# FFN weights quantized in their final work space, later modulation rows in two stages, sigmoid ahead of the small loads, new fill and drain orders

## The reference, cut to what matters

```python
mod = (_silu(L0_c) @ L0_wmod).reshape(B, 6, 1, -1)
sa, ca, ga, sb, cb, gb = (mod[:, i] for i in range(6))
ga = (2 * (ga >= 0) - 1) * max(abs(ga), 0.25)        # gb likewise
h = _layernorm(x) * (1 + ca) + sa
x = x + ga * rwkv_two_layers(h)     # each layer: _time_mix (wkv scan over 4096 tokens), then _channel_mix
h = _layernorm(x) * (1 + cb) + sb
x = x + gb * fp4_ffn(h)             # gate, up, down, inputs and weights quantized in blocks of 16
...
# fp4_quant_dequant(w): scale = max|block| / 6, values rounded to {0, .5, 1, 1.5, 2, 3, 4, 6}, times scale
```

## Time and profile before

| | us |
|---|---|
| median of 3 runs | 2996.9 (2995.78 to 2999.09) |
| profiled execution, its own time | 2993.3 |
| its span | 2991.6 |
| PE busy in the span | 2765.8 (92%) |
| DVE, ACT, POOL busy | 2360.4, 1382.2, 1283.5 |

### The profile page before, as it was taken

One profiled execution on the slowest core, in us unless ns is written; L12 is line 12 of the kernel. 1 busy time (PEld: TensorE's weight loads), 2 busy tenths in 40 slices (PEclk: granted clock), 3 DMA queues, 4 the chain that ended last, 5 costly groups with the idle time before them and its releaser, 6 DMA issues.

```text
span 2991.6 us, 78855 instructions
## 1 busy us (share of the span) xinstructions
PE 2765.8 (92%) x32829; PEld 2201.4 (74%) x32829; DVE 2360.4 (79%) x5345; ACT 1382.2 (46%) x2771; POOL 1283.5 (43%) x1457
## 2 busy tenths in 40 slices
PE   5789999999999999999999999999999999999875
PEld 3567777777777777777777777777777777777653
DVE  5756888888888888888888888888888888888664
ACT  1344444544454454455445545545554444454331
POOL 3344444445444444544444444444444444444320
PEclk7789999999999999999999999999999999999997
DMA  4000000000000000000000000000000000000000
GB/s 149 14 5 9 13 12 5 9 12 12 12 12 12 5 9 13 12 12 12 12 5 12 9 12 12 12 12 9 9 9 12 12 12 12 5 9 12 8 8 7
DMA packets 36831, 41.51 MB, mean 14 GB/s; under 512 B 3272, under 2 KB 35200, under 8 KB 36480
## 3 DMA queue, kind: packets, MB, share of 16 engines
...
## 4 chain that ended last, share of the span: by engine, by line
PE 61%; DVE 22%; ACT 8%; issue 5%; POOL 3%; ACTq 0%; DVEq 0%; DMA 0%; POOLq 0%
PE ps_all L1444 10%; PE ps_all L1256 9%; PE ps_all L1264 8%; PE ps_all L1458 6%; PE ps_all L1495 5%; PE ps_all L1477 5%; PE ps_all L1362 4%; DVE sxrk L1125 3%; DVE att L1131 2%; PE ps_all L1248 2%; DVE stats L1023 2%; ACT mixin L911 2%; DVE chan L1069 2%; PE ps_all L1294 2%; PE ps_all L1388 1%
## 5 line engine op out<-in xcount | busy, mean ns | idle before, releaser
L753 POOL TENSOR_TENSOR mixin<-mixin,hT_tm 128x512 f32<-128x512 f32 x320 | 390.3, 1230 | 354.5 <-DVE mixin L1090 354.3
L1444 PE MATMUL ps_all<-chan,cwk 128*128 128x256 f32 x1536 | 374.7, 390 | 8.3 <-DVE chan L1069 5.4
L1125 DVE TENSOR_TENSOR sxrk<-sxrk,dec 128x512 f32<-128x512 f32 x384 | 273.9, 713 | 97.0 <-PE ps_all L1362 93.9
L1458 PE MATMUL ps_all<-cwv,chan 128*128 128x256 f32 x1536 | 343.3, 380 | 0.0
L1444 PEld LDWEIGHTS ps_all<-chan,cwk 128*128 128x128 f32 x1536 | 283.4, 191 | 63.2 <-issue 20.3
L1458 PEld LDWEIGHTS ps_all<-cwv,chan 128*128 128x128 f32 x1536 | 290.1, 191 | 38.6 <-ACT chan L853 0.3
L733 POOL TENSOR_TENSOR rstd<-var,powc 128x2 f32<-128x2 f32 x224 | 188.3, 841 | 241.1 <-DVE var L1029 240.1
L1090 DVE SCALAR_TENSOR_TENSOR mixin<-ps_all,vcol,sxrk 128x256 f32<-128x256 f32 x640 | 269.9, 475 | 21.1 <-PE ps_all L1294 10.9
L1362 PEld LDWEIGHTS ps_all<-sxrk 64*64 64x64 f32 x10240 | 170.1, 130 | 137.5 <-issue 137.4
L1362 PE MATMUL ps_all<-sxrk 64*64 64x32 f32 x10240 | 202.8, 217 | 43.1 <-DVE att L1131 39.8
L772 POOL TENSOR_TENSOR lora<-S,dec 128x256 f32<-128x256 f32 x128 | 91.1, 712 | 352.0 <-DVE S L1140 351.3
...
## 6 DMA issues: line engine op xcount, KB each, us to landing
xin<-in_L_attn_x_dram SPq DMA_DIRECT2D x32, 256.0 KB, 2.7
tok<-in_L_attn_x_dram SPq DMA_DIRECT2D x32, 256.0 KB, 2.7
out_dram<-x SPq DMA_DIRECT2D x32, 256.0 KB, 2.1
...
```

Source lines behind the costliest of these rows:

```text
L753: pool.tensor_tensor(m, m, hT["tm", l][:, :, :, 1:P + 1].rearrange("p k c t -> p (k c) t"), ALU.add).then_inc(ev["mixed"][b], 1)
L1125: v.tensor_tensor(rko, rko, t, ALU.mult).then_inc(ev["rk_lev"][b], 1)
L1444: ins = pe.matmul(bank(b, "ck", lj, "k")[:, m * TT:(m + 1) * TT], cwk[:, l, k, n:n + P], k_in[:, k, :], start=(k == 0), stop=(k == KC - 1))
L1458: ins = pe.matmul(bank(b, "cv", l, "v")[:, c * D:(c + 1) * D], relu[t // 2][:, t % 2, c * P:(c + 1) * P], cwv[:, l, t, :], start=(t == 0), ...
```

## The change

The repeated middle (`ORDER`) stays as it is. What changes is the prologue, stream 5, and the order tables of the first five and the last three blocks:

- ACT first evaluates a sigmoid of a constant column, then the sigmoid of c, and only then issues the 14 small loads and ln_out_w.
- PE runs six matmuls of the identity (`PRELUDE`) before the first modulation matmuls.
- `mods` becomes two stages, one for each sequence (`mods.0`, `mods.1`), on the two shared PSUM banks 6 and 7; each has eight matmul instructions and eleven DVE operations.
- The raw FFN weights are loaded into three parts of ffn_work and normalized and rounded there, with downT as the other operand; tok[1], mixin[1], sxrk[1] and xres[1] are no longer used. The loads of up and down follow on SP behind the last modulation matmul (before: behind `norm` of the matrix before).
- Five zero fills for S, att and tm_w2b and four for hT move from POOL to DVE; the one for downT to DVE after the last `grid`.
- `HEAD` and `TAIL` have new orders on all engines.

```diff
     streams.append(s + [("dn", 0)])
-    streams.append([("mods", 0), ("centre", 0), ("norm", 0), ("abs", 0), ("grid", 0), ("centre", 1), ("norm", 1), ("abs", 1),
+    streams.append([("mods", 0), ("mods", 1), ("centre", 0), ("norm", 0), ("abs", 0), ("grid", 0), ("centre", 1), ("norm", 1), ("abs", 1),
                     ("grid", 1), ("norm", 2), ("abs", 2), ("grid", 2)])
...
+        if kind == "mods":
+            for k in SHARED:
+                place((0, "weights", L + 1, arg, k), (k,))
...
-        raw = flat(tok[1])
-        su_norm, su_magic = flatmix[1][:, 0:IT * D], sxrk[1][:, 0:IT * D]
-        su_out = [ffn_work[:, g * IT * D:(g + 1) * IT * D] for g in range(3)]
+        raw = [ffn_work[:, n * IT * D:(n + 1) * IT * D] for n in (2, 0, 1)]
+        su_magic = flat(downT)
...
+            for b in range(B):
+                for k in SHARED:
+                    filled(sp, 0, "weights", L + 1, b, k)
+            raw_rows("L0_ffn_w_up", 1)
...
             for l in range(L):
-                pool.memset(att[l][:, :, :, :], 0.0).then_inc(su_pool, 1)
-                pool.memset(S[l][:, :, :, :, :], 0.0).then_inc(su_pool, 1)
...
+            act.wait_ge(su_pool, 4)
+            act.activation(csilu[:, 0:1], powc[:, 0:1], ACT.Sigmoid).then_inc(su_act, 1)
+            act.wait_ge(c_loaded, 16)
+            act.activation(csig[:, :], vcol[:, NV:NV + B * KC], ACT.Sigmoid).then_inc(su_act, 1)
             for n, name in enumerate(VECS):
...
+            for l in range(L):
+                for kind in ("tm", "cm"):
+                    v.memset(hT[kind, l][:, :, :, P:P + 1], 0.0).then_inc(zeroed, 1)
+                v.memset(S[l][:, :, :, :, :], 0.0).then_inc(zeroed, 1)
...
             def weights_norm(i, b, g):
-                v.wait_ge(raw_loaded, (32, 64, 80)[g])
-                quant_norm(v, raw, SETS[g], su_amax, su_scl, su_over, su_rcp, su_neg, su_norm, suq_wait(g), suq)
+                v.wait_ge(raw_loaded[g], (32, 32, 16)[g])
+                if g:
+                    v.wait_ge(suq["q_out"], g)
+                quant_norm(v, raw[g], SETS[g], su_amax, su_scl, su_over, su_rcp, su_neg, raw[g], suq_wait(g), suq)
...
+            pe.wait_ge(consts, 1)
+            for _ in range(PRELUDE):
+                pe.matmul(ps[SHARED[1]][:, 0:P], ident[:, :], ident[:, :], start=True, stop=True)
...
-            def mods(i, b_, _):
+            def mods(i, b_, b):
                 pe.wait_ge(mod2_loaded, 16 * KC)
-                for b in range(B):
-                    mod_rows(b, 1)
-                pe.wait_ge(mod_step, MOD_FIRST)
-                mod_rows(0, 2)
-                mod_rows(1, 2).then_inc(su_pe, 1)
+                for j, to in enumerate(SHARED):
+                    fill(pe, 0, "weights", L + 1, b, to)
```

The tables read, where stream 5 and 6 stand among the stages of tile 0 and 1 on DVE:

```diff
-    DVE: """0/0 lna.in lnb.in h0 lna.tm lnb.tm mix; 0/5 centre.0; 0/0 mf.0 mf.1 mf.3; 0/5 mods; 0/0 mf.2 mf.4; 0/5 norm.0; 0/0
-        lev.1 lev.2; 0/5 grid.0; 0/0 lev.3 pg lev.4 lev.5 lev.6 st.0 st.1 gna gnb; 0/5 centre.1 norm.1; 0/0 wo; 0/2 lna.cm
+    DVE: """0/0 lna.in lnb.in h0 lna.tm lnb.tm mix; 0/5 centre.0 mods.0; 0/0 mf.0 mf.1 mf.3 mf.2 mf.4 lev.1 lev.2; 0/5 mods.1; 0/0
+        lev.3 pg lev.4 lev.5 lev.6; 0/5 norm.0; 0/0 st.0 st.1 gna gnb; 0/5 grid.0 centre.1 norm.1; 0/0 wo; 0/2 lna.cm lnb.cm;
```

More of the change, by code:

```diff
@@ new lines @@
+    AC: """0/0 turn.tm mix pw1 pk pr pw2 pv pg kt; 0/5 abs.0; 0/0 gna yt; 0/2 turn.cm; 0/5 abs.1; 0/6 wt.0.0 wt.0.1; 1/0 turn.tm;
+        0/2 ck.0 ck.1; 1/0 mix; 0/2 ck.2 cr; 0/5 abs.2; 1/0 pw1 pk pr pw2 pv; 0/1 turn.tm; 0/6 wt.1.0; 1/0 pg; 0/1 mix; 0/6
+        wt.1.1; 1/0 kt; 0/1 pw1 pk pr; 1/0 gna; 0/1 pw2; 1/0 yt; 0/6 wt.2.0 wt.2.1 wt.2.2; 0/1 pv; 1/2 turn.cm; 0/1 pg; 1/2
+        ck.0; 2/0 turn.tm; 1/2 ck.1; 2/0 mix; 1/2 ck.2 cr; 0/1 kt gna; 2/0 pw1 pk pr; 0/1 yt; 2/0 pw2 pv; 0/3 turn.cm; 1/1
+        turn.tm; 2/0 pg; 1/1 mix; 0/3 ck.0; 1/1 pw1 pk pr; 0/3 ck.1""",
@@ new lines @@
+    POOL: """0/0 lna.in lna.tm mix mf.0 mf.1 mf.3 mf.2 mf.4 tot st.0 st.1 gnb yt; 0/2 lna.cm; 1/0 lna.in; 0/2 cmix; 1/0 lna.tm mix
+        mf.0 mf.1 mf.3 mf.2; 0/2 cv; 1/0 mf.4; 0/1 lna.tm; 1/0 tot st.0; 0/1 mix mf.0 mf.1 mf.3 mf.2; 1/0 st.1 gnb yt; 0/1
+        mf.4 tot st.0; 1/2 lna.cm cmix; 2/0 lna.in lna.tm mix mf.0 mf.1; 0/1 st.1; 2/0 mf.3; 0/1 gnb yt; 2/0 mf.2; 1/2 cv; 2/0
+        mf.4 tot; 1/1 lna.tm; 0/3 lna.cm cmix; 1/1 mix mf.0 mf.1 mf.3 mf.2; 2/0 st.0 st.1 gnb; 1/1 mf.4 tot; 2/0 yt; 0/3 cv;
+        2/2 lna.cm; 3/0 lna.in lna.tm; 2/2 cmix; 3/0 mix""",
@@ L220, in stage_name @@
         return f"{kind}.{arg[1]}"
-    if kind in ("centre", "norm", "abs", "grid"):
+    if kind in ("mods", "centre", "norm", "abs", "grid"):
         return f"{kind}.{arg}"
@@ L612, in turns, with mod_bank @@
                 steps[kind](i, b, arg)
-        def mod_bank(b, j):
-            return ((3, 5, 3), (4, 6, 4))[b][j]
+        def mod_bank(b):
+            return BANKS[1][b]
         def first(i):
@@ L941, in _ @@
         def _(v):
-            v.wait_ge(su_act, 1)
+            for l in range(L):
+                for kind in ("tm", "cm"):
+                    v.memset(hT[kind, l][:, :, :, P:P + 1], 0.0).then_inc(zeroed, 1)
+                v.memset(S[l][:, :, :, :, :], 0.0).then_inc(zeroed, 1)
+            for c in range(NC):
+                v.memset(tm_w2b[(2 * c + 1) * E:(2 * c + 2) * E, :, :], 0.0).then_inc(zeroed, 1)
+            v.memset(att[0][:, :, :, :], 0.0).then_inc(zeroed, 1)
+            v.wait_ge(su_act, 2)
             v.wait_ge(c_loaded, 16)
@@ new lines, in mods @@
+                for k in SHARED:
+                    filled(v, 0, "weights", L + 1, b, k)
+                done = MOD_FIRST + b * MOD_EACH
+                v.tensor_copy(rows[:, b, 3, :], later[3]).then_inc(mod_step, 1)
+                v.tensor_scalar(rows[:, b, 4, :], later[4], 1.0, None, ALU.add).then_inc(mod_step, 1)
+                for n in (2, 5):
+                    v.tensor_scalar(sign, later[n], 0.0, 2.0, ALU.is_ge, ALU.mult).then_inc(mod_step, 1)
+                    v.tensor_scalar(size, later[n], -1.0, 0.25, ALU.mult, ALU.max).then_inc(mod_step, 1)
+                    v.wait_ge(mod_step, done + (4 if n == 2 else 9))
+                    v.tensor_tensor(size, later[n], size, ALU.max).then_inc(mod_step, 1)
+                    v.wait_ge(mod_step, done + (5 if n == 2 else 10))
+                    v.scalar_tensor_tensor(rows[:, b, n, :], sign, -1.0, size, ALU.add, ALU.mult).then_inc(mod_step, 1)
+                    if n == 2:
+                        v.wait_ge(mod_step, done + 6)
+                        v.tensor_tensor(rows[:, b, n, :], rows[:, b, n, :], lnout, ALU.mult).then_inc(mod_step, 1)
@@ L988, in mods @@
+                v.wait_ge(mod_step, done + MOD_EACH)
+                for k in SHARED:
                     v.sem_inc(free[k], 1)
@@ L1216, in _, with mods @@
             pe.wait_ge(consts, CONSTS)
-            def mods(i, b_, _):
+            def mods(i, b_, b):
                 pe.wait_ge(mod2_loaded, 16 * KC)
-                for b in range(B):
-                    mod_rows(b, 1)
-                pe.wait_ge(mod_step, MOD_FIRST)
-                mod_rows(0, 2)
-                mod_rows(1, 2).then_inc(su_pe, 1)
+                for j, to in enumerate(SHARED):
+                    fill(pe, 0, "weights", L + 1, b, to)
+                    for k in range(KC):
+                        ins = pe.matmul(ps[to][:, :], csilu_row[b][k], wmod[k][:, (j + 1) * 2 * D:(j + 2) * 2 * D], start=(k == 0), stop=(k == KC - 1))
+                    ins.then_inc(full[to], 1)
             def weights_turn(i, b, gn):
```

343 lines of the change are left out of this document (152 added, 191 removed).

## The result

| | before | after |
|---|---|---|
| median, us | 2996.9 (2993.13 to 3001.22, 9 runs) | 3001.57 (2999.78 to 3009.69, 9 runs) |
| ratio after to before | | 1.0023, 95% interval 1.0015 to 1.0031 |
| profiled execution, own time and span | 2993.3, 2991.6 | 3006.37, 3004.6 |
| PE busy | 2765.8 | 2775.5 |

What follows compares the result with a forecast made beforehand. PE and its order were taken to bound the middle, DVE to decide the first 130 us. Terms along tile 0 left a 1.5 us gain at wo, the rest counted nothing: 2993.3 to 2991.8 profiled, median 2995.4, range 2986 to 3001.

Steps and rivals of the forecast that it cites:

- The permuted rest of the fill and the drain: New stage orders after the first tile and at the end: counted as nothing, bounds taken from PE's idle time there.
- the slower rival: Fill: quantization on DVE overlaps POOL, ten times 0.78 us against +1.5; 6.3 us slower, 3003.2; chance 0.12.
- Sigmoid first: Prologue: sigmoid 3.9 us earlier, small tables issued behind it land at 13.6, lnb.in at 14.6; +3.0 us.
- Two stages: Tile 0's modulation split: mix at 26.3, mf.0 at 30.8 (+4.9); with mods.1 later, lev.3 at 56.4 (+7.3).
- the favourable bound: Tile 0 before lev.3: pv at the full clock takes half of 3.78 us, 1.9 us more gain.
- norm.0 behind lev.6: DVE, tile 0: norm.0 takes 5.3 us before st.0, which starts at 69.4; -2.4 us, leaving +4.9.
- the forecast's own bound of 6.0: Start through tile 0's wo: favourable tables (+1.5), pv (+1.9) and mods.0 (+1.1) give 6.0 us earlier.
- a sign of being wrong: DVE's wo of tile 0 well before 86, or PE's idle time after 130 us falling by more than 3 us.
- Middle: 330 to 2750 us: bound by PE and its order, left alone by the change.
- the fill gains all: Head gains 6.0 us at full clock, new lists recover another 3 to 6 from 130 to 330; 2988; chance 0.36.
- nothing arrives: Prologue: tables land 6.4 us after issue, so 1.3 us later than before, 2998.2; chance 0.12.
- PE busy from 130 to 330 as before: Check in the window after the start: PE's busy time should stay as before, there and from 2750 on.

Runs made afterwards that it cites:

- the exchanged lists: Old or new early part, fill order from 126 us and drain order recombined between the kernel before and the changed one; ratios to before 0.9994 to 1.0027.
- the tables-first one: New early part with both old orders, but ACT issues the small tables and ln_out_w ahead of the sigmoids; 2994.64 us, ratio 0.9999 to the kernel before.
- two more items: New fill order only behind 290 us, with turn.cm, PE's yt and DVE's cv put back to their old places; 2992.84 us, 0.9994 to the kernel before.

## Why the prediction was wrong

The step that failed is the one that was priced at nothing: "The permuted rest of the fill and the drain: nothing, with bounds from the idle time that is there." The bounds, too, looked only for a gain. By the ratios of the exchanged lists the early part gains 0.0006, the new fill behind it costs 0.0027 and the new drain 0.0002: -1.8 + 8.1 + 0.6 = 6.9 us, the 1.0023 of the result. Of the fill 5.7 us sit behind 205 us. Exchanged in another order the parts come out differently, the early part at 1.2 to 3.3 us (1.0027 to 1.0023; 1.0009 to 0.9998) and the drain at 0.6 to 2.7; each step carries some 4 us of noise, and only the fill's is clear of it. I had read the 22.4 us that PE idles from 130 to 330 us as room for improvement, and not that the same idle time shows how close DVE's results come to PE's need for them: a DVE item moved back can turn into a PE wait, and then into low clock. The PE clock column there (0.93) was the warning, and I used it as evidence that PE is nearly fed. The measured 3001.57 lies close to the slower rival's 3003.2 by chance, since that rival's cause is not what the runs show.

By steps, in the profiled executions:

- Sigmoid first: +3.0 forecast, lnb.in +1.2 (17.63 to 16.46). The first sum was right (sigmoid at 4.35) and on the safe side (matmuls done at 9.5, not 11.7); the prelude ended at 5.17, after c was there and not before it, and the matmuls followed at 5.27. The tables were mis-sized: the last is issued at 9.67 and the transpose waits for it until 15.01, 5.0 us after issuing ended, instead of the 3.6 taken. It lies inside the bounds (6.4). The remaining 0.5 us lies between the transpose and lnb.in (1.45 us, 0.94 taken). The Trainium skill, "DMA: Bandwidth & Descriptors", section "Anatomy of one DMA", with its nearly constant 2.0 us, given there for a DMA issued by GpSimd, would have given 12.0; the trace says 15.0 beside 94 GB/s of weight traffic.
- Two stages: mix at 28.04 (26.3 forecast), mf.0 at 32.98 (30.8), both late by about what lnb.in was late (1.9). lev.3 at 57.58 (56.4): +6.1 for +7.3; pv ran at the full clock as in the favourable bound (1.99). mf.4 came behind 8.87 us of idle DVE, "some 8".
- norm.0 behind lev.6: st.0 at 69.31 (69.4). DVE's wo at 86.81 with no wait before it (87.9): +2.6 for +1.5; 0.8 of the difference is norm.1's last operation, which took 1.76, not 2.56. This pair of profiles flatters the forecast: fifteen further profiled kernels with the new early part (all but the tables-first one) reach that wo at 84.2 to 86.5, the three with the old one (before, its new lists, its new drain) at 89.4 to 91.7. The means, 85.5 over the sixteen with the new part and 90.8 over the three, are 5.3 us apart, near the forecast's own bound of 6.0. Twelve of the sixteen lie ahead of 86, by up to 1.9 us, which touches what the prediction named as a sign of being wrong. So the early part was priced too low by these profiles; the times show only 1.2 to 3.3 us of it.
- Middle, "the change leaves it alone": true for the order; a lag or lead carries through it, with the drift given at the end.
- The rival "the fill gains all": lev.1 of tile 1 at 125.87 instead of 128.78 and the means above support its first half, the new lists did the reverse of its second. The rival "nothing arrives" had a right cause (tables late, by 1.4 of its 2.8 us), but the tile gained all the same.
- The slower rival named the wrong place. Of the quantization's operations two are longer than their likes, 2.09 and 2.57 us instead of 1.62 at 118.32 and 120.44, beside a POOL addition at 118.89: 1.4 us instead of the 7.8. The Trainium skill, "GPSIMD Engine Reference", section "Specifications", says that the two engines contend where DVE reads two inputs from SBUF; these rows agree, but overlap is rare, and not every one lengthens DVE: grid.0's last operation at 78.52 overlapped POOL's from 79.20 on and took its usual 1.76, while POOL's took 2.20 instead of 1.26.
- "PE busy from 130 to 330 as before" was named as the check: 176.10 against 177.64 looks like it. The count (2293 against 2354) and the clock show the loss, the busy time hides it.

What stays open: how the 5.7 us divide over single items. The swap of one turn explains 0.7 us of the last stretch, and with two more items 1.1, in profiles and not in times; the late `2/2 cmix` on DVE is read from the rows and was not tried by itself. Nor is it shown what the part from 126 to 205 us costs. The best kernels found, the new early part with the old lists or nearly them, stand at 0.9992 to 0.9994 in four variants, each interval just reaching 1.0: probably 2 us faster than before.
